# Interleaving the three copies of a q/k operand in DRAM, so that one transfer fetches them

## The reference

```
h = layernorm(x) * (1 + ca) + sa
q, k, v = split(h @ W_attn + b_attn)          # 16 heads of 16
phi(u) = exp(u @ omega - 0.5 * sum(u * u)) / sqrt(128)      # omega is 16 x 128, u is q or k scaled by 1/4
y_t = phi(q_t) . cumsum(phi(k) v^T) / (phi(q_t) . cumsum(phi(k)) + 1e-6)
x = x + ga * (y @ W_proj + b_proj)
h = layernorm(x) * (1 + cb) + sb
x = x + gb * ffn(h)                           # 4 experts, top 2, shared weights 256 -> 1024 -> 256 plus a rank-4 term
```

## Time and profile before

| | |
|---|---|
| median of 3 runs | 756.73 us (754.6 to 759.03) |
| profiled execution | 757.15 us, its span 754.8 us |
| mean granted TensorE clock | 0.995 of full speed |
| TensorE busy | 733.7 us (97%) |
| VectorE, ScalarE, GpSimd busy | 516.6, 428.1, 73.5 us |
| moved by DMA | 62.66 MB, mean 83 GB/s |

### The profile page before, as it was taken

How to read it: one execution, slowest core, us unless ns; L and a number is a source line. 1 busy time by engine, 2 the same in 40 slices (tenths; PEclk the granted TensorE clock), 3 DMA queues, 4 the chain that set the end, 5 groups by cost and what they waited for, 6 DMA issues and landing times.

```text
span 754.8 us, 16910 instructions
## 1 busy us (share of the span) xinstructions
PE 733.7 (97%) x6080; PEld 592.9 (79%) x6080; DVE 516.6 (68%) x1254; ACT 428.1 (57%) x775; POOL 73.5 (10%) x82
## 2 busy tenths in 40 slices
PE   7899999999999999999999999999999999999797
PEld 4678769887788878887698877987788876888466
DVE  6547777577766776677766776757766777656566
ACT  5677455765566636665556655575456655665232
POOL 0560200002000110001000020000200010000200
PEclk9999999999999999999999999999999999999999
DMA  9850570106410273104701065101741028100000
GB/s 309 227 120 2 156 167 15 42 28 196 96 56 0 83 173 64 56 0 131 185 4 56 28 179 113 43 13 35 200 85 56 0 101 190 29 30 3 27 1 29
DMA packets 33929, 62.66 MB, mean 83 GB/s; under 512 B 3694, under 2 KB 17874, under 8 KB 33842
## 3 DMA queue, kind: packets, MB, share of 16 engines
q1 hardware_dynamic: 33334, 61.09, 30.3%
q10 hardware_dynamic: 576, 1.31, 0.5%
HBM read 40.37 MB, written 22.02 MB: 83 GB/s over the span
## 4 chain that ended last, share of the span: by engine, by line
PE 91%; DVE 3%; DMA 2%; ACT 1%; SPq 1%; issue 0%; POOL 0%; ACTq 0%; POOLq 0%; DVEq 0%
PE pa L546 13%; PE ring L679 12%; PE prod L559 8%; PE ring L525 6%; PE pa L421 5%; PE pa L422 5%; PE pa L423 5%; PE ring L579 4%; PE pa L666 4%; PE ring L530 3%; PE ring L768 2%; PE ring L586 2%; PE prod L546 2%; PE ring L701 2%; PE ring L760 2%; PE prod L525 2%
## 5 line engine op out<-in xcount | busy, mean ns | idle before, releaser
L1213 DVE TENSOR_TENSOR am_phk<-pa,const 128x512 f32<-128x512 f32 x112 | 77.0, 689 | 43.5 <-PE pa L546 42.8
L546 PE MATMUL pa<-phq,phkT 128*128 128x128 f32 x768 | 101.3, 275 | 0.0
L546 PEld LDWEIGHTS pa<-phq,phkT 128*128 128x128 f32 x768 | 95.3, 191 | 2.3 <-DVE am_phk L1213 0.2
L1393 DVE SCALAR_TENSOR_TENSOR am_phk<-ring,am_phk 128x512 f32<-128x512 f32 x64 | 44.1, 690 | 47.7 <-PE ring L768 47.7
L525 PE MATMUL ring<-xq,omega_x 100*128 100x512 f32 x198 | 71.1, 439 | 3.2 <-DMA xq<-norm_parts 2.2
L939 ACT ACTIVATE phq<-ring 128x512 f32<-128x512 f32 x84 | 50.6, 602 | 40.2 <-PE ring L525 39.2
L422 PE MATMUL pa<-wo_r,qk_l 128*128 128x256 f32 x248 | 69.7, 281 | 0.0
L421 PE MATMUL pa<-wo_r,qk_r 128*128 128x256 f32 x248 | 69.7, 281 | 0.0
L423 PE MATMUL pa<-wo_l,qk_r 128*128 128x256 f32 x248 | 69.6, 281 | 0.0
L1019 ACT ACTIVATE qk_r<-phq 128x512 fp32r<-128x512 f32 x64 | 40.5, 633 | 49.2 <-DVE phq L1399 49.2
L939 ACT ACTIVATE phkT<-ring 128x512 f32<-128x512 f32 x98 | 58.3, 595 | 13.3 <-PE ring L525 12.9
(11 more groups left out here) (208 smaller groups left out, 1616.1 us busy)
## 6 DMA issues: line engine op xcount, KB each, us to landing
xq<-qk_parts SPq DMA_DIRECT2D x45, 512.0 KB
qk_parts<-qk_r SPq DMA_DIRECT2D x32, 256.0 KB, 4.0
qk_parts<-qk_l SPq DMA_DIRECT2D x32, 256.0 KB, 4.6
xr<-in_L_attn_x SPq DMA_DIRECT2D x8, 512.0 KB, 3.4
out_x<-tg SPq DMA_DIRECT2D x16, 256.0 KB, 2.2
tok<-in_L_attn_x SPq DMA_DIRECT2D x7, 512.0 KB, 3.3
phq<-in_L_wmod SPq DMA_DIRECT2D x2, 512.0 KB, 7.2
am_phk<-in_wi_columns SPq DMA_DIRECT2D x2, 512.0 KB, 8.9
```

What stands on the lines that cost most here:

```text
L546: mm = pe.matmul(score_bank(q, a)[:, tt], phkT[:, q % 2, a, tt], query(q)[:, a, tt], start=True, stop=True)
L1213: dve.tensor_tensor(am[:, 2 * (q % 2) + a, :].rearrange("p (c t) -> p c t", c=NT), score_bank(q, a)[:].rearrange("p (c t) -> p c t", c=NT) ...
L1393: dve.scalar_tensor_tensor(r2[:, f % 2, :], z_bank[f % 4][:], 0.0, rho, ALU.max, ALU.mult).then_inc(r2_done.sem, 1)
```

## The change

The operand's rows are interleaved: row r of a pair's 32 has its three copies in rows 3r, 3r+1 and 3r+2 of `xq`, not in r, r+32 and r+64. `parts_out` is laid out so that the three copies of a row follow each other; then the 96 rows have one constant stride in DRAM, and one transfer fetches them. For that the rounded part is sent twice: three sends of 256 KB for each part j instead of two. The two rounded copies are sent when ScalarE has written them (`sq_ready`), the low part after the split. `omega_x` has its rows in the same order; since its low rows are now every third one, `setup_omega` makes them by two instructions over all 100 rows, a multiplication by a column of signs and a multiply-add with a column of ones and zeros, which come as two more columns of the constants. The counts of the semaphores follow.

```diff
@@ counts @@
-        qk_out = [sig(name, 4 * 16) for name in ("qk0_out", "qk1_out")]
+        qk_out = [sig(name, 2 * COPIES * 16) for name in ("qk0_out", "qk1_out")]
-        moved = [sig(name, 4 * 16) for name in ("moved0", "moved1")]
+        moved = [sig(name, 2 * 16) for name in ("moved0", "moved1")]
@@ SP @@
             def send(n, j):
-                wait(sp, qk_split, n, j + 1)
-                for part, src in enumerate((qk_r, qk_l)):
-                    sp.dma_start(parts_out[part, j // 2, :, j % 2], src[:, j, :].bitcast(F32)).then_inc(qk_out[j // 2].sem, 16)
+                wait(sp, sq_ready, n, j + 1)
+                for copy, src in enumerate((qk_r, qk_r, qk_l)):
+                    if copy == 2:
+                        wait(sp, qk_split, n, j + 1)
+                    sp.dma_start(parts_out[j // 2, :, copy, j % 2], src[:, j, :].bitcast(F32)).then_inc(qk_out[j // 2].sem, 16)
             def fetch_qk(n, half, pairs, signal):
                 wait(sp, qk_out[half], n, qk_out[half].per)
-                for copy, part in enumerate((0, 0, 1)):
-                    src = parts_out[part, half].rearrange("(i r) k t -> r i (k t)", r=PAIR_ROWS)[:, pairs]
-                    sp.dma_start(xq[copy * PAIR_ROWS:(copy + 1) * PAIR_ROWS, half, pairs]
-                                 .rearrange("r i k t -> r i (k t)").bitcast(F32), src).then_inc(signal.sem, 16)
+                src = parts_out[half].rearrange("(i r) o k t -> (r o) i (k t)", r=PAIR_ROWS)[:, pairs]
+                sp.dma_start(xq[0:COPIES * PAIR_ROWS, half, pairs].rearrange("r i k t -> r i (k t)").bitcast(F32),
+                             src).then_inc(signal.sem, 16)
@@ TensorE, features @@
-                        pe.wait_ge(lead_moved[0].sem, 4 * 16)
+                        pe.wait_ge(lead_moved[0].sem, 2 * 16)
-                        pe.wait_ge(lead_moved[1].sem, 3 * 16)
+                        pe.wait_ge(lead_moved[1].sem, 16)
@@ VectorE, setup_omega @@
                 dve.tensor_copy(omega_x[:], om_f).then_inc(om_high.sem, 1)
                 dve.wait_ge(om_high.sem, 1)
-                dve.tensor_tensor(omega_x[low, :], om_f[low, :], omega_x[low, :].bitcast(F32),
-                                  ALU.subtract).then_inc(om_done.sem, 1)
+                dve.wait_ge(ld_const.sem, 16)
+                dve.tensor_scalar(omega_x[:], omega_x[:].bitcast(F32), om_sign[0:XROWS, 0:1], None,
+                                  ALU.mult).then_inc(om_high.sem, 1)
+                dve.wait_ge(om_high.sem, 2)
+                dve.scalar_tensor_tensor(omega_x[:], om_f, om_sign[0:XROWS, 1:2], omega_x[:].bitcast(F32),
+                                         ALU.mult, ALU.add).then_inc(om_done.sem, 1)
@@ DRAM @@
-    parts_out = nc.dram_tensor("qk_parts", (2, 2, P, 2, T), F32, kind="Internal").ap()
+    parts_out = nc.dram_tensor("qk_parts", (2, P, COPIES, 2, T), F32, kind="Internal").ap()
```

More of the change, by code:

```diff
@@ L53 @@
 PAIR_ROWS = 2 * DH
-XROWS = 3 * PAIR_ROWS + 4
+COPIES = 3
+XROWS = COPIES * PAIR_ROWS + 4
 LORA = E * R
@@ L85 @@
 F32R = mybir.dt.float32r
-CONSTS = {"ident": P, "causal": P, "headsum": VA, "prio": E, "expert": 2}
+CONSTS = {"ident": P, "causal": P, "headsum": VA, "prio": E, "expert": 2, "om_sign": 2}
 class Signal:
@@ L120, in build @@
             at += width
-        ident, causal, headsum, prio, expert = (cols[name] for name in CONSTS)
+        ident, causal, headsum, prio, expert, om_sign = (cols[name] for name in CONSTS)
         wa_r, wa_l = sb("wa_r", [P, KT, 3 * C], F32R), sb("wa_l", [P, KT, 3 * C], F32R)
@@ L343, in fetch_norms @@
                 src = norms_out[half, :, :, pairs].rearrange("q a i k t -> (q a) (i k t)")
-                sp.dma_start(xq[3 * PAIR_ROWS:XROWS, half, pairs].rearrange("r i k t -> r (i k t)").bitcast(F32),
+                sp.dma_start(xq[COPIES * PAIR_ROWS:XROWS, half, pairs].rearrange("r i k t -> r (i k t)").bitcast(F32),
                              src).then_inc(signal.sem, 16)
@@ L1099, in setup_omega @@
             def setup_omega():
-                low = slice(PAIR_ROWS, 2 * PAIR_ROWS)
                 dve.wait_ge(ld_om.sem, 16)
@@ L1586, in constants @@
     expert = np.stack([r % 32 < LORA, r % 32 >= LORA], 1).astype(np.float32)
-    consts = np.concatenate([ident, causal, headsum, prio, expert], 1)
+    low_row = (r < COPIES * PAIR_ROWS) & (r % COPIES == 1)
+    om_sign = np.stack([np.where(low_row, -1, 1), low_row], 1).astype(np.float32)
+    consts = np.concatenate([ident, causal, headsum, prio, expert, om_sign], 1)
     rows = np.zeros((XROWS, 2 * M), np.float32)
@@ L1590, in constants @@
         for a in range(2):
-            rows[3 * PAIR_ROWS + 2 * part + a, a * M:(a + 1) * M] = -0.5
+            rows[COPIES * PAIR_ROWS + 2 * part + a, a * M:(a + 1) * M] = -0.5
     return {"consts": np.ascontiguousarray(consts), "norm_rows_padded": rows}
@@ L1602, in laid_out @@
     omega = rows['norm_rows_padded'].copy()
-    for k in range(3):
+    for copy in range(COPIES):
         for a in range(2):
-            omega[k * PAIR_ROWS + a * DH:k * PAIR_ROWS + (a + 1) * DH, a * M:(a + 1) * M] = rows['L0_attn_omega']
+            at = copy + COPIES * a * DH
+            omega[at:at + COPIES * DH:COPIES, a * M:(a + 1) * M] = rows['L0_attn_omega']
     return {
```

## The result

The changed kernel takes 761.89 us (median of 14 runs, 758.73 to 764.75), the kernel before 756.92 us on the same chips (14 runs, 754.53 to 759.80). The ratio is 1.0066 with a 95% interval of 1.005 to 1.0083: slower by 3.8 to 6.3 us. The forecast was 757.0 us with a range to 760.2.

A forecast was written before the change was run, and what follows sets the result against it. TensorE, busy 97% of the span, was taken to bound the kernel. Start-up +0.2 and loop +0.2 on 757.15 us gave 757.55; runs' median 0.4 lower gave 757.1, stated as 757.0, range 753.4 to 760.2.

The forecast's parts named there:

- The forecast there: Start-up: first feature matmul at 30.65 + 0.05 against 30.50, so +0.2 us; low -0.7, high +2.2.
- Loop: 0: Seven loop passes: added DMA work lies beside TensorE's; 0, with +0.2 for small shifts, -0.5 if two waits go.
- rival C: Loop: merged fetch behind the norms' fetch makes it late, 0.5 us in each of seven passes, +3.5, 760.4 us; chance 0.13.
- the four times: Whole kernel: the forecast's 757.0 us and the three rivals' 754.0, 760.4 and 759.0 us.
- The queue idle earlier: Loop, at the norms' fetch: sends add 1.3 us, a half's fetch is 2.5 us faster, so the queue idles earlier.
- rival D: Merged fetch stays at 203 GB/s: start-up +0.7, loop up to 0.3 us a pass, +1.5, 759.0 us; chance 0.17.
- one and a half times the 32-row rate: Fetch data: by the port rule 96 rows run this fast, lead fetch 1.3 us; 300 GB/s taken.
- Sends: Start-up: two more 256 KB transfers take 1.3 us, last landing from 25.04 to 26.35; bounds nothing to 2.8 us.
- Fetch issue: Start-up, SP: one issue of 0.43 us replaces three, without the odd 1.57 us; norms' fetch at 26.84 instead of 27.48.
- Landing of the norms: Start-up: norms land 1.95 us after the lead fetch's end at 28.7, so 30.65 instead of 30.45; low 29.8.
- Setup of omega: Start-up, VectorE: 0.33 us more ahead of the norms' split, covered until the norms' fetch with 0.2 us left; bounds 0.2 to 0.9.
- Clock: After the start-up: with TensorE's pause as long as before, the fall to 0.50 from 33.4 to 36.8 us stays, 1.7 us lost.

The follow-up runs named there:

- e3: Changed kernel, SP issuing the second half's merged fetch only once the first half's norms have landed; 759.06 us, ratio 1.0028.
- e12: Changed kernel with the wait for the norms ahead of the merged fetch, omega's rows made later, and paired norm sends; 757.87 us, ratio 1.0014.
- e11: Kernel before with both norm parts in one tile, two norm sends per half instead of four; 755.87 us, ratio 0.9985.
- e2: Changed kernel without the second rounded send from the second block on (stale rows fetched), merged fetch kept; 761.21 us, ratio 1.0059.
- e14: Kernel of e2 with its 96 rows fetched by three transfers of 32 rows, low rows first; 760.18 us, ratio 1.0043.
- e1: Kernel before with the added traffic alone: rounded part sent twice and early, three 32-row fetches kept; 760.18 us, ratio 1.0040.
- e13: Kernel before with early sends, the rounded part sent twice in the first block only; 759.87 us, ratio 1.0037.
- e5: Kernel before with only the two instructions of the new setup_omega, signs laid out for old rows; 759.19 us, ratio 1.0023.
- e4: Kernel before with the rounded part sent early, at sq_ready, once; 758.43 us, ratio 1.0016.
- e6: Kernel of e3 with setup_omega moved behind the first block's norm split; 758.40 us, ratio 1.0018.

## Why the prediction was wrong, step by step

**Where the time went.** In the two profiles 3.8 us lie between the spans: 3.76 in the loop, 0.25 in the start-up, 0.2 given back at the end. Between the medians of the runs it is 5.0 us, between the means 4.9, and the runs put more of it in the start-up than the pair of profiles does. The forecast there was +0.2 us; e3 is 2.1 us above before and e12 2.0 above e11, each with a loop that is as fast as its partner's. So the start-up costs about 2 us (in e3 with the wait of pass 1, 0.66 us, in it), with intervals about as wide, and the 0.25 is only what these two profiles happen to show. Part of the whole can be clock. Granted clock short of 1, times the span, averages 6.1 us over the runs of the changed kernel; for the kernel before, whose clock is on record only beside the experiments, the four sets average 3.5, 4.6, 4.7 and 5.3 us. It is not the cause in e12, whose runs have 4.4 where e11's have 4.8.

**Loop: 0.** This step failed. It rested on two reasons. The first was that "the norms stand first in the queue in both kernels". They do, and e2, e3 and e14 show that this isn't enough: the transfer over 96 rows, issued 0.3 us behind the norms', delays their landing by about half a microsecond (4.26 us in the mean of the changed kernel's seven passes and 4.41 in e2, against 3.78 in e3 with nothing behind it). This is rival C, mechanism, place and price: 0.5 us in each of seven passes was its forecast, 4.1 us of waits more than before were measured, and 760.4 us was the nearest of the four times. It had 0.13. Its own row spoke for it: where two of seven passes already wait, the margin is nothing, and every tenth counts in full.

**The queue idle earlier.** The second reason was the size "a half's fetch faster by 2.5 us", from 300 GB/s. Measured are 226 to 227 GB/s (328 in one stretch of 1 us at the start of a transfer), 7 to 12% above the thirds, near the low bound that the prediction wrote down. With that, rival D's step holds: the queue's end moves into the norms' sends, which e1 shows by itself (first gap 2.8 to 3.1 us, 1.4 us in seven passes; D had up to 0.3 a pass). The sentence on one and a half times the 32-row rate, taken from the Trainium skill ("SBUF — State Buffer", Door 1: The DMA port swizzle), isn't borne out either: 1.07 to 1.12 times was measured.

**Sends.** Right in itself: 26.35 forecast, 26.5 in e13 and 26.87 in e14. In the changed kernel other work gates the fetch: it is issued at 26.15, right behind the last norms' send, and the norms' fetch at 27.31, when that send has landed.

**Fetch issue.** 0.43 us forecast, 0.31 to 0.33 measured, and the odd 1.57 us is gone. It isn't tied to the three fetches, though: e13 issues three in 1.23 us, while one of e14's takes 1.52.

**Landing of the norms.** 30.65 and a matmul at 30.70 forecast, 30.75 measured, but by another path: the norms' fetch waited for its own sends (0.47 us later than the 26.84 of the working) and then took 3.40 us. A right number by wrong steps.

**Setup of omega.** 0.33 us forecast, 0.43 in the trace. The cover of two tenths is used up, as the step feared: the three instructions are in the chain, and the landing of the norms' sends gates the fetch. The step put the price at nothing as long as the cover lasts; e5, which has these instructions alone, is 2.0 us above before (0.2 to 3.3). The 1.7 us that the step took for a landing is an upper bound only, since in the kernel before the fetch at 101.15 stands straight behind SP's eighth send (the last pair is issued from 100.48, 0.63 us), whether or not the norms had landed earlier.

**Clock.** The fall stays, as forecast: TensorE's granted clock is 0.51, the lower level, from 33.6 to 37.1 us. But the reason given, a pause as long as before, doesn't hold: the pause was 0.7 us instead of 2.2. And e12 has the same pause (0.73 us) and no fall:

```profile
33.00:37.00 4.00, 4.00 (x33) 3.87 (x33) 1.71 (x5) 2.17 (x5) 3.84 (x4) 1.00 0.99 345
```

So the length of this pause alone doesn't decide it, and no run shows what does. The profile of the changed kernel has two more falls, 0.57 from 13 to 17 us and 0.50 around 721 us:

```profile
13.00:17.00 4.00, 4.00 (x13) 2.58 (x14) 2.23 (x4) 3.92 (x8) 0.00 (x0) 0.57 1.05 316
...
33.60:37.10 3.50, 3.50 (x19) 3.50 (x19) 1.01 (x3) 1.08 (x2) 3.34 (x4) 0.51 1.02 360
...
720.50:722.50 2.00, 2.00 (x3) 0.95 (x4) 1.29 (x2) 0.91 (x2) 0.00 (x0) 0.50 0.00 0
```

The one at 13 us stands behind a pause of 3.33 us, in which TensorE waits for ScalarE's `tok` up to 12.96; before, that pause is 1.92 us and no fall follows. A late load of x (VectorE's statistics wait for it until 8.64 us, 7.10 before) is not enough for it: in e3 and e14 they wait until 8.94 and 8.65, TensorE has no such pause and its clock stays at 1.00. The one in the last block is in the profile of before too (0.50 from 716.5 to 719.5 us), and in ten of the 17 profiles. These ten take 116.2 to 116.5 us from the first feature load of the seventh pass to the end, the other seven 114.8 to 115.4, whatever the edit. From 60 to 700 us the clock is 1.00 in all of them, so the loop's waits owe nothing to it. Runs with a lower clock are the longer ones (of the changed kernel, 764.75 us at 0.987 and 758.73 at 0.997). Such falls go with the spread of 5 us among runs of one kernel, and they are why the start-up's share can't be split further: e4, e5 and e6 differ from before by 1 to 2 us, each with an interval as wide. What is left open, then: which part of the start-up costs the 2 us, how much is clock, and why one transfer over 96 rows delays the norms more than three of 32 do.

**Range.** It ended at 760.2, because C and D were priced one at a time. They share their place, so both can hold; their waits overlap rather than add, and with the start-up they still end 1.7 us above it.

## What to carry to other kernels

A small transfer that gates an engine has to be guarded against what is issued behind it as well as ahead of it: issue the big one once the small one has landed (e3), or in pieces (e14). A margin that already shows a wait in some passes is a margin of zero, and every edit near it should be priced per pass. One fetch in place of three saves 0.9 us of a queue's issue time that nobody waited for in the loop; 13% more bytes (71.05 MB instead of 62.66), where the queue was full, held up the small sends behind them by 0.1 to 0.4 us a pass (e1). And one profile of each kernel is not enough for a start-up: a difference of 1 or 2 us there needs the times of many runs, and a partner that differs in nothing else.

## What was not expected of the hardware

- A fetch into 96 rows moves 226 to 227 GB/s where fetches into 32 rows move 203 to 212 and sends from 128 rows 391 to 408.
- A fetch into 4 rows lands 3.57 to 4.06 us after its issue with nothing behind it (seven passes of e3, by SP's own wait). With three 32-row fetches behind it the loads that waited for it started at up to 4.1 us in before and e14 and up to 4.4 in e4 and e5; with one into 96 rows, at 4.1 to 4.7 us in the changed kernel and 4.2 to 4.6 in e2.
- The granted clock fell to 0.50 for 3.3 us after a pause of 2.4 us (e13), and to 0.51 for 3.5 us after one of 0.7 us (changed kernel); in e11 and e12, whose pauses at the first features were 0.5 and 0.7 us, it stayed at 1.00, in e11:

```profile
33.00:37.00 4.00, 4.00 (x29) 3.77 (x30) 1.71 (x4) 2.35 (x5) 3.84 (x4) 1.00 0.87 297
```
